# Experts' scales on GpSimd with a power, ahead of placing; totals between the halves of the Gram products

## The chip, the cores and the metric

The kernel runs on one core of a Trainium2 chip. A core has TensorE (PE in the profile, its weight loads PEld), VectorE (DVE), ScalarE (ACT), GpSimd (POOL) and SyncE (SP), each with a queue of its own, and 16 DMA engines. The engines wait for each other by semaphores. The metric is the device time of one execution in microseconds (us), and the median of the runs is compared.

## The reference

Eight batches of 512 tokens, 256 wide, go through a layer norm and an attention whose queries and keys are normed over tokens, so that it can be computed by products of 256x256; then through a layer norm and a mixture of eight experts (two chosen for each token, hidden width 1024) beside a shared layer.

```python
# attention, per batch: x is 512 x 256
Q = x @ Wq.T + bq; K = x @ Wk.T + bk; V = x @ Wv.T + bv
Q = transpose(_l2_norm(Q)); K = _l2_norm(K)
tailor_sum = 1.0 / (L + einsum('bnc,bc->bn', Q, sum(K, axis=-1) + EPS))
matrix = einsum('bmn,bcn->bmc', K, V)
matrix_sum = value_sum + einsum('bnm,bmc->bcn', Q, matrix)
x + gamma * matrix_sum * tailor_sum[:, None, :]
# experts
topk_w, topk_idx = top_k(softmax(flat @ gate_W), 2)
out = 0.5 * gelu(flat @ shared_W + shared_b)
for e in range(8):
    h = gelu(flat @ W1[e] + b1[e])
    out = out + combine[:, e:e + 1] * (h @ W2[e] + b2[e])
```

Each half is followed by a layer norm and added to its input.

## The kernel before

The front part, up to about 230 us, is a software pipeline of steps -1 to 7. In step s batch s+1 enters (layer norm, Gram matrix of its normed tokens), batch s is mixed (256x256 products from the Gram matrix, key and query norms, the mixing matrix), batch s-1 leaves (the attention's result is normed and added, split in a high and a low half of 16 bits, turned, and sent through the shared layer and the gate), batch s-2 is placed (its tokens are counted by expert and get slots in a table), and expert s is prepared. Each engine runs its part of a step in a written order: `step(s)` in the block of that engine, and `last_step()` for step 7.

An expert is prepared so. ScalarE squares W2 (`w2_square`, L1368) and W1 (`w1_square`, L1375) with sums per partition. TensorE adds these over the partitions with one small product of ones (`totals`, L1065, in the bank of the key norms). ScalarE copies the three totals out (`totals_out`, L1352). VectorE makes bounds of them (`expert_bounds`, L1729 to L1732, the last a reciprocal), ScalarE takes the root (`expert_scales`, L1383), and VectorE masks it to a power of two (L1739) and writes the expert's entries of the table `tab` (`expert_tables`, L1740 to L1743). With the scales ScalarE writes the high halves of W2 (`w2_highs`, L1395) and W1 (`w1_highs`, L1389), and VectorE the low halves (`w2_lows`, L1752, and `w1_lows`, L1748). These four each run over 128x2048 elements.

Around them stand, on TensorE: `weigh` (L977, L981), `count` (L1077, L1079), `key_norms` (L990), `cosines` (L998), `totals`, `grams` (L958, 16 matmuls into two halves of a bank), `mix` (L1006), the turning of the leaving tokens (L1043), the shared layer (L534 to L536, L1058), `turn_mix` (L1014), `turn_x` (L967) and `attend` (L1023). `attend` waits for `mixT_out` (L1664) on VectorE, which comes after `w1_lows`. On ScalarE, `spread` (L1272) takes the root for a layer norm, `xf_high` (L1332) writes the high half of the leaving tokens, `xfT_out` (L1338) copies half of the turned ones. On VectorE, `leave` (L1686, L1691) norms the leaving tokens, `xf_low` (L1696) writes their low half, and at the end of step 6 `first_chosen` (L1762 on) reads the places after five batches; it waits for `first_placed`, which GpSimd raises in `keep_places` (L793).

GpSimd places: `place` (L779 to L788) is a chain of 14 small operations, each waiting for the one before; `keep_places` copies the result from batch 4 on; `write_slots` issues indirect DMAs (L797, eight for a batch) into the table. In its queue the batches 0 to 5 follow one another, with the gathers (L811) of blocks 0 and 1 ahead of batch 5 and of blocks 2 and 3 behind it. The blocks' tokens are later turned (L1091) and sent through the experts (L534 to L536 with gelu L1515).

## Time and profile before

| | |
|---|---|
| median of 3 runs | 725.46 us |
| lowest and highest run | 725.3 and 730.57 us |
| the profiled execution's own time | 731.88 us |
| its span, first to last instruction | 730.1 us |
| busy: TensorE, its weight loads | 606.3, 513.5 us |
| busy: VectorE, ScalarE, GpSimd | 465.1, 445.9, 321.3 us |
| mean granted clock of TensorE, as a share of full speed | 0.942 |

A row of a timeline gives the start and the duration of an instruction (or of a few alike, "xN") in us from the start of the span, then engine, source line, operation, output and inputs by name, and shapes. In square brackets stands how long the engine had been idle before it, and what ended that.

### The profile page before, as it was taken

The page shows a single profiled execution, that of the slowest core. Times are in us where ns is not written, and L with a number is a line of the kernel's source. Part 1 is how long each engine was busy: PE and PEld are TensorE (multiplying, and loading weights), DVE is VectorE, ACT ScalarE, POOL GpSimd, SP SyncE. Part 2 cuts the span into 40 slices and gives each one's busy share as a digit, 9 for nine tenths or more (in the row PEclk, how much of TensorE's full clock was granted, in tenths as well). Part 3 has the DMA queues.
Part 4 walks back from the last instruction along what each step waited for, and adds up shares of the span by engine and source line. Part 5 has one row for each costly group of instructions (what it writes and reads, how often), then busy time and mean ns, then how long its engine had stood idle before and what let it go on. Part 6 is the DMA issues. An engine that isn't in the chain of part 4 may idle for free.

```text
span 730.1 us, 16808 instructions
## 1 busy us (share of the span) xinstructions
PE 606.3 (83%) x4903; PEld 513.5 (70%) x4903; DVE 465.1 (64%) x1242; ACT 445.9 (61%) x875; POOL 321.3 (44%) x435
## 2 busy tenths in 40 slices
PE   4778888788867898977969989999999999999400
PEld 3656677677656787855848777889888988888300
DVE  5479899989886545422438766644444445678884
ACT  2657767766745765533635676857656656578743
POOL 4000435645347232644752422334334447674676
PEclk9989999999988999988989999999999999999855
DMA  7553664451453321112112311122212139743438
GB/s 255 181 208 124 192 200 131 160 174 60 123 209 134 99 98 40 48 34 60 53 30 72 94 43 59 46 74 88 75 45 61 44 82 193 155 81 74 98 125 166
DMA packets 45272, 78.25 MB, mean 107 GB/s; under 512 B 16962, under 2 KB 30596, under 8 KB 44804
## 3 DMA queue, kind: packets, MB, share of 16 engines
q1 hardware_dynamic: 33492, 48.19, 20.6%
q0 software_dynamic: 11696, 28.98, 16.5%
q8 instruction: 47, 0.77, 0.5%
q14 instruction: 37, 0.30, 0.2%
HBM read 48.17 MB, written 28.98 MB: 106 GB/s over the span
## 4 chain that ended last, share of the span: by engine, by line
PE 54%; DVE 20%; issue 11%; ACT 6%; another core or an unknown queue 3%; POOL 2%; DMA 2%; DVEq 1%; ACTq 0%; POOLq 0%; SPq 0%
PE banks L534 13%; PE banks L536 12%; PE banks L535 12%; PE banks L1023 3%; PE banks L1193 2%; ACT X L1515 2%; PE banks L958 2%; DVE W L1748 2%; PE banks L1091 2%; DVE W L1752 2%; DVE stage L1981 1%; PE banks L1006 1%; PE banks L981 1%; PE banks L977 1%
## 5 line engine op out<-in xcount | busy, mean ns | idle before, releaser
L1515 ACT ACTIVATE X<-banks,b1T,tab 128x256 f32<-128x256 f32 x256 | 129.2, 554 | 126.7 <-PE banks L536 91.1
L822 POOL DMA_INDIRECT y_rows<-X,tb x72 | 80.6, 1119 | 208.6 <-DVE X L2012 193.5
L1981 DVE SCALAR_TENSOR_TENSOR stage<-X,tab,stage 128x512 f16<-128x512 f32 (+1 forms) x160 | 108.4, 696 | 99.3 <-ACT stage L1521 80.0
L534 PE MATMUL banks<-W,stage 128*128 x576 | 159.7, 277 | 12.0 <-issue 8.6
L536 PE MATMUL banks<-W,stage 128*128 x576 | 159.9, 278 | 5.6 <-issue 5.3
L535 PE MATMUL banks<-W,stage 128*128 x576 | 159.6, 277 | 2.1 <-issue 1.8
L534 PE MATMUL banks<-X,W 128*128 128x256 f16 x512 | 141.5, 276 | 8.8 <-DVE X L1995 7.6
L536 PE MATMUL banks<-X,W 128*128 128x256 f16 x512 | 141.2, 276 | 1.4 <-issue 1.4
L535 PE MATMUL banks<-X,W 128*128 128x256 f16 x512 | 141.3, 276 | 0.3 <-issue 0.3
L1521 ACT ACTIVATE stage<-X,tab 128x512 f16<-128x512 f32 (+1 forms) x160 | 107.1, 679 | 10.7 <-ACT X L1515 6.7
L797 POOL DMA_INDIRECT table<-pay,slot_i x64 | 73.1, 1142 | 58.6 <-PE banks L1023 37.3
L811 POOL DMA_INDIRECT X<-xf_rows,tb x72 | 76.2, 1058 | 32.8 <-issue 21.3
L534 PEld LDWEIGHTS banks<-W,stage 128*128 128x128 f16 x576 | 57.1, 99 | 24.3 <-issue 17.6
L535 PEld LDWEIGHTS banks<-W,stage 128*128 128x128 f16 x576 | 57.2, 99 | 14.3 <-issue 7.0
L536 PEld LDWEIGHTS banks<-W,stage 128*128 128x128 f16 x576 | 57.2, 99 | 12.1 <-issue 5.1
L534 PEld LDWEIGHTS banks<-X,W 128*128 x512 | 50.7, 99 | 17.0 <-issue 10.5
L1995 DVE COPY X<-banks 128x1024 f16<-128x1024 f16 x36 | 24.8, 689 | 57.7 <-remote 50.9
L536 PEld LDWEIGHTS banks<-X,W 128*128 x512 | 50.8, 99 | 9.0 <-issue 2.5
L535 PEld LDWEIGHTS banks<-X,W 128*128 x512 | 50.7, 99 | 6.3
L2005 DVE SCALAR_TENSOR_TENSOR X<-banks,tab,zone 128x512 f32<-128x512 f32 (+1 forms) x39 | 26.7, 694 | 31.0 <-PE banks L536 27.6
L779 POOL TENSOR_TENSOR rank<-counts,zone 128x32 f32<-128x32 f32 x8 | 2.7, 338 | 75.5 <-ACT counts L1358 74.7
L1515 ACT ACTIVATE X<-X,b1T,tab 128x128 f32<-128x128 f32 x64 | 26.4, 483 | 15.6 <-DVE X L1987 15.5
(300 smaller groups left out, 1149.7 us busy)
## 6 DMA issues: line engine op xcount, KB each, us to landing
stage<-in_L_ffn_W SPq DMA_DIRECT2D x10, 1024.0 KB
W<-in_L_ffn_W SPq DMA_DIRECT2D x6, 1024.0 KB, 8.7
X<-in_L_attn_x SPq DMA_DIRECT2D x8, 512.0 KB, 5.5
out<-X SPq DMA_DIRECT2D x8, 512.0 KB
...
```

Of the source, the lines that this page charges most:

```text
L534: pe.matmul(o, lh, rh, start=first, stop=False)
L535: pe.matmul(o, lh, rl, start=False, stop=False)
L536: return pe.matmul(o, ll, rh, start=False, stop=last)
L797: g.indirect_dma_start(out=table, out_offset=bass.IndirectOffsetOnAxis(ap=slot_i[:, b, k, t:t + 1], axis=0), in_=pay[:, b, t, k, :], in_of ...
L811: g.indirect_dma_start(out=xg[:, j % 2 * HALVES + h, :], out_offset=None, in_=xf_rows[0:FIRST * C, :] if j < EARLY else xf_rows, in_offset ...
L822: g.indirect_dma_start(out=y_rows, out_offset=bass.IndirectOffsetOnAxis(ap=tb[:, j % ROWS, h, 1:2], axis=0), in_=y32[:, j % 2 * HALVES + h ...
L1023: mm = pe.matmul(Z_PS[:, t, :], xT[b % 2][:, f, t * P:(t + 1) * P], mixT[:, f, :], start=(f == 0), stop=(f == NF - 1))
L1515: a.activation(tile, tile if joint(j) else PS[m][:, r * BT:(r + 1) * BT], ACT.Gelu, bias=b1T[:, bass.ds(e * NH + 2 * m + r, 1)], scale=tab ...
L1521: a.activation(hhl[:, j % 2, 2 * m:2 * m + 2, 0, span(j, p)], h32[:, m % 2, :].rearrange("p (r n) -> p r n", r=2)[:, :, span(j, p)], ACT.C ...
L1981: v.scalar_tensor_tensor(o[1], src, tab[:, 1, bass.ds(e, 1)], o[0], ALU.mult, ALU.subtract).then_inc(h_low, 1)
L1995: v.tensor_copy(xbT[:, q * NF * 2:(q + 1) * NF * 2, :].rearrange("p a n -> p (a n)"), PS[4][:, :].bitcast(F16)).then_inc(xb_ready, 1)
L2005: v.scalar_tensor_tensor(yq, PS[5 + j % 2][:, :].rearrange("p (h d) -> p h d", h=HALVES)[:, p:p + n, :], tab[:, 2, bass.ds(e, 1)], b2e[:, ...
```

## The change

The scales of expert i move from VectorE and ScalarE to GpSimd. `expert_tables(i)` there is a chain of eleven small operations: the totals are scaled, one `pow` with exponent -0.5 takes the place of reciprocal and root, and a conversion to an integer and back takes the place of the mask. Experts 0 and 1 come ahead of all placing, expert b+2 ahead of `place(b)` for b = 0 to 4, and expert 7 ahead of the first two gathers. ScalarE's splits wait for the seventh operation of the chain. On TensorE the totals' product moves from ahead of the Gram products to between their two halves, in steps 0 to 6. On ScalarE the root `spread(2, ...)` goes ahead of the totals' copy.

```diff
--- before.py
+++ after.py
@@ -22,8 +22,9 @@
 NORMS, TAILOR = 3, 3
 SETUP_V = 14
 LOW_ROW = 32
-EV_BOUNDS, EV = 4, 9
+EV_MASKED, EV = 7, 11
 EXP_MASK = 0x7F800000
+EXP_ONE = float(0x00800000)
 EXP_FLIP = float(0x7F000000)
 BT = 256
 HALVES = BT // P
@@ -124,6 +125,7 @@
         ebnd = sb("ebnd", [P, 4], F32)
         escl = sb("escl", [P, 4], F32)
         einv = sb("einv", [P, 4], F32)
+        eexp = sb("eexp", [P, 4], I32)
         tab = sb("tab", [P, 3, E], F32)
         slot_i = sb("slot_i", [P, B, 2, T], I32)[:, :, :, :]
         pay = sb("pay", [P, B, T, 2, 4], I32)[:, :, :, :, :]
@@ -792,6 +793,28 @@
                 g.wait_ge(placed, PLACES * (b + 1))
                 g.tensor_copy(place_then[:, b - FIRST + 1, :], place_of).then_inc(first_placed, 1)
 
+            def expert_tables(i):
+                e = TURN[i]
+                g.wait_ge(totals_ready, i + 1)
+                g.wait_ge(w1_low, i)
+                g.wait_ge(w2_low, i)
+                settle(g)
+                link = chain(g, expert_steps, EV * i)
+                g.tensor_scalar(ebnd[:, 0:2], etot[:, 0:2], 1e-24, 1.0 / TOP / TOP, ALU.max, ALU.mult).then_inc(expert_steps, 1)
+                link.count[0] += 1
+                link(g.tensor_scalar(ebnd[:, 2:3], etot[:, 0:1], float(D), None, ALU.mult))
+                link(g.tensor_tensor(ebnd[:, 2:3], ebnd[:, 2:3], etot[:, 2:3], ALU.add))
+                link(g.tensor_scalar(ebnd[:, 2:3], ebnd[:, 2:3], 2.0 / TOP / TOP, 1e-24 / TOP / TOP, ALU.mult, ALU.max))
+                link(g.tensor_tensor(escl[:, 0:3], ebnd[:, 0:3], eps[:, 3:4].broadcast_to([P, 3]), ALU.pow))
+                link(g.tensor_scalar(eexp[:, 0:3], escl[:, 0:3].bitcast(I32), 1.0 / EXP_ONE, -0.5, ALU.mult, ALU.add))
+                link(g.tensor_scalar(escl[:, 0:3].bitcast(I32), eexp[:, 0:3], EXP_ONE, None, ALU.mult))
+                assert link.count[0] == EV_MASKED
+                link(g.tensor_scalar(einv[:, 0:3].bitcast(I32), escl[:, 0:3].bitcast(I32), -1.0, EXP_FLIP, ALU.mult, ALU.add))
+                link(g.tensor_scalar(tab[:, 0, e:e + 1], einv[:, 0:1], 1.0 / SX, None, ALU.mult))
+                link(g.tensor_copy(tab[:, 1, e:e + 1], escl[:, 2:3]))
+                link(g.tensor_tensor(tab[:, 2, e:e + 1], einv[:, 1:2], einv[:, 2:3], ALU.mult))
+                assert link.count[0] == EV
+
             def write_slots(b, t):
                 for k in range(2):
                     g.indirect_dma_start(out=table, out_offset=bass.IndirectOffsetOnAxis(ap=slot_i[:, b, k, t:t + 1], axis=0),
@@ -822,12 +845,17 @@
                     g.indirect_dma_start(out=y_rows, out_offset=bass.IndirectOffsetOnAxis(ap=tb[:, j % ROWS, h, 1:2], axis=0),
                                          in_=y32[:, j % 2 * HALVES + h, :], in_offset=None).then_inc(y_stored[j % 2], 16)
 
+            expert_tables(0)
+            expert_tables(1)
             g.wait_ge(table_init, 16)
             for b in range(B - 2):
                 if b + 3 == B:
                     g.wait_ge(cosines_ps, B)
+                    expert_tables(E - 1)
                     gather(0)
                     gather(1)
+                if b + 3 < B:
+                    expert_tables(b + 2)
                 place(b)
                 if b >= FIRST - 1:
                     keep_places(b)
@@ -948,15 +976,16 @@
             mm.then_inc(wqk_turned, 1)
             pe.wait_ge(consts_set, 6)
 
-            def grams(b):
+            def grams(b, lo=0, hi=NF):
                 pe.wait_ge(xs_ready, T * (b + 1))
                 pe.wait_ge(gram_ready, b)
                 pe.wait_ge(u_ready, past(T * (b - 2)))
                 pe.wait_ge(counts_ready, past(b - 2))
-                for i in range(NF):
+                for i in range(lo, hi):
                     for t in range(T):
                         mm = pe.matmul(GRAM_PS[:, i * D:(i + 1) * D], xs[:, t, i * P:(i + 1) * P], xs[:, t, :], start=(t == 0), stop=(t == T - 1))
-                mm.then_inc(gram_ps, 1)
+                if hi == NF:
+                    mm.then_inc(gram_ps, 1)
 
             def turn_x(b, f):
                 pe.wait_ge(xs_ready, T * (b + 1))
@@ -1101,10 +1130,12 @@
                 if mixing is not None:
                     key_norms(mixing)
                     cosines(mixing)
+                if entering is not None:
+                    grams(entering, 0, 1)
                 if i is not None:
                     totals(i)
                 if entering is not None:
-                    grams(entering)
+                    grams(entering, 1, NF)
                 if mixing is not None:
                     mix(mixing)
                 if leaving is not None:
@@ -1375,21 +1406,14 @@
                 a.activation(w1_part(slot(i), 0), staged(i, 0), ACT.Square, accum_out=essq[:, 0:1]).then_inc(w1_squares, 1)
                 a.activation(bsq[:, :], b1T[:, TURN[i] * NH:(TURN[i] + 1) * NH], ACT.Square, accum_out=essq[:, 2:3]).then_inc(w1_squares, 1)
 
-            def expert_scales(i):
-                a.wait_ge(expert_steps, EV * i + EV_BOUNDS)
-                a.wait_ge(w1_low, i)
-                a.wait_ge(w2_low, i)
-                settle(a)
-                a.activation(escl[:, 0:3], ebnd[:, 0:3], ACT.Sqrt, scale=TOP * TOP).then_inc(expert_roots, 1)
-
             def w1_highs(i):
-                a.wait_ge(expert_steps, EV * i + EV_BOUNDS + 1)
+                a.wait_ge(expert_steps, EV * i + EV_MASKED)
                 a.wait_ge(w1_squares, 2 * (i + 1))
                 settle(a)
                 a.activation(w1_part(slot(i), 0), staged(i, 0), ACT.Copy, scale=escl[:, 0:1]).then_inc(w1_high, 1)
 
             def w2_highs(i):
-                a.wait_ge(expert_steps, EV * i + EV_BOUNDS + 1)
+                a.wait_ge(expert_steps, EV * i + EV_MASKED)
                 a.wait_ge(w2_squares, i + 1)
                 settle(a)
                 a.activation(w2_part(slot(i), 0), staged(i, 1), ACT.Copy, scale=escl[:, 1:2]).then_inc(w2_high, 1)
@@ -1414,14 +1438,12 @@
                     w1_square(i)
                 if mixing is not None:
                     q_roots(mixing)
+                if leaving is not None:
+                    spread(2, x1_dev, (x1_mean, T * (leaving + 1)), 0, 1.0 / SX / SX)
                 if i is not None:
                     totals_out(i)
-                if leaving is not None:
-                    spread(2, x1_dev, (x1_mean, T * (leaving + 1)), 0, 1.0 / SX / SX)
                 if mixing is not None:
                     cosines_out(mixing)
-                if i is not None:
-                    expert_scales(i)
                 if leaving is not None:
                     xf_high(leaving)
                 if entering is not None:
@@ -1486,7 +1508,6 @@
                 spread(2, x1_dev, (x1_mean, T * b), 0, 1.0 / SX / SX)
                 cosines_out(b)
                 totals_out(E - 1)
-                expert_scales(E - 1)
                 xf_high(b - 1)
                 mix_scale(b)
                 w1_highs(E - 1)
@@ -1551,6 +1572,7 @@
             spread(2, x1_dev, (x1_mean, T * B), 0, 1.0 / SX / SX)
             a.preload_act_table(ACT.Gelu)
             a.wait_ge(blocks_ready, 1)
+            a.wait_ge(expert_steps, EV * E)
             gelu(0, 0, 2)
             xf_high(B - 1)
             gelu(0, 2, 4)
@@ -1722,27 +1744,6 @@
                 v.tensor_tensor(both, pick[b % 2][0], pick[b % 2][1], ALU.add).then_inc(both_ready, 1)
                 v.tensor_tensor(gap[b % 2], best[1], best[0], ALU.subtract).then_inc(gap_ready, 1)
 
-            def expert_bounds(i):
-                link = chain(v, expert_steps, EV * i)
-                v.wait_ge(totals_ready, i + 1)
-                v.wait_ge(expert_roots, i)
-                link(v.scalar_tensor_tensor(ebnd[:, 2:3], etot[:, 0:1], float(D), etot[:, 2:3], ALU.mult, ALU.add))
-                link(v.tensor_scalar(ebnd[:, 0:2], etot[:, 0:2], 1e-24, None, ALU.max))
-                link(v.tensor_scalar(ebnd[:, 2:3], ebnd[:, 2:3], 2.0, 1e-24, ALU.mult, ALU.max))
-                link(v.reciprocal(ebnd[:, 0:3], ebnd[:, 0:3]))
-                assert link.count[0] == EV_BOUNDS
-
-            def expert_tables(i):
-                e = TURN[i]
-                link = chain(v, expert_steps, EV * i + EV_BOUNDS)
-                v.wait_ge(expert_roots, i + 1)
-                link(v.tensor_scalar(escl[:, 0:3].bitcast(I32), escl[:, 0:3].bitcast(I32), EXP_MASK, None, ALU.bitwise_and))
-                link(v.tensor_scalar(einv[:, 0:3].bitcast(I32), escl[:, 0:3].bitcast(I32), -1.0, EXP_FLIP, ALU.mult, ALU.add))
-                link(v.tensor_scalar(tab[:, 0, e:e + 1], einv[:, 0:1], 1.0 / SX, None, ALU.mult))
-                link(v.tensor_copy(tab[:, 1, e:e + 1], escl[:, 2:3]))
-                link(v.tensor_tensor(tab[:, 2, e:e + 1], einv[:, 1:2], einv[:, 2:3], ALU.mult))
-                assert link.count[0] == EV - EV_BOUNDS
-
             def w1_lows(i):
                 v.wait_ge(w1_high, i + 1)
                 v.scalar_tensor_tensor(w1_part(slot(i), 1), staged(i, 0), escl[:, 0:1], w1_part(slot(i), 0), ALU.mult, ALU.subtract).then_inc(w1_low, 1)
@@ -1882,12 +1883,8 @@
                     x1_stats(leaving)
                 if mixing is not None:
                     inverses(mixing)
-                if i is not None:
-                    expert_bounds(i)
                 if leaving is not None:
                     leave(leaving)
-                if i is not None:
-                    expert_tables(i)
                 if mixing is not None:
                     tailor_factors(mixing)
                 if leaving is not None:
@@ -1920,8 +1917,6 @@
                 inverses(b)
                 tailor_factors(b)
                 leave(b - 1)
-                expert_bounds(E - 1)
-                expert_tables(E - 1)
                 tailor(b)
                 mix_out(b)
                 xf_low(b - 1)
@@ -2071,6 +2066,7 @@
 
             attended(B - 1)
             residual(B - 1)
+            v.wait_ge(expert_steps, EV * E)
             turned_block(0)
             x1_stats(B - 1)
             w2_lows(E - 1)
```

The order of the instructions on GpSimd, where the first batch is placed: before, the program has placing alone there (L779 to L788) and the eight table writes.

```order
L763 IOTA pay 128x64
L779 TENSOR_TENSOR rank<-counts,zone 128x32
L780 TENSOR_TENSOR zone<-zone,counts 128x8
L782 TENSOR_TENSOR zone<-pick,rank 128x32
L767 TENSOR_TENSOR zone<-zone 128x16
```

After the change the table of expert 2 stands there, behind those of experts 0 and 1 (`ebnd`, `escl`, `eexp`, `einv` are its steps, 3 numbers for each partition; the power is L808).

```order
L803 TENSOR_SCALAR ebnd<-counts 128x2
L805 TENSOR_SCALAR ebnd<-counts 128x1
L806 TENSOR_TENSOR ebnd<-ebnd,counts 128x1
L807 TENSOR_SCALAR ebnd<-ebnd 128x1
L808 TENSOR_TENSOR escl<-ebnd,eps 128x3
L809 TENSOR_SCALAR eexp<-escl 128x3
L810 TENSOR_SCALAR escl<-eexp 128x3
L812 TENSOR_SCALAR einv<-escl 128x3
L813 TENSOR_SCALAR tab<-einv 128x1
L814 COPY tab<-escl 128x1
L815 TENSOR_TENSOR tab<-einv 128x1
L780 TENSOR_TENSOR rank<-counts,zone 128x32
```

All of placing, and the table writes behind it, have moved behind these eleven. On VectorE, from the reciprocal of the norms to the low half of the leaving tokens, before:

```order
L1638 RECIPROCAL rk<-kn 128x4
L1729 SCALAR_TENSOR_TENSOR ebnd<-counts 128x1
L1730 TENSOR_SCALAR ebnd<-counts 128x2
L1731 TENSOR_SCALAR ebnd<-ebnd 128x1
L1732 RECIPROCAL ebnd<-ebnd 128x3
L1686 RECIPROCAL cf<-sd 128x4
L1691 TENSOR_SCALAR zone<-X,mv,cf 128x256 x4
L1739 TENSOR_SCALAR escl<-escl 128x3
L1740 TENSOR_SCALAR einv<-escl 128x3
L1741 TENSOR_SCALAR tab<-einv 128x1
L1742 COPY tab<-escl 128x1
L1743 TENSOR_TENSOR tab<-einv 128x1
```

and after, where lines have moved by 17 to 22:

```order
L1660 RECIPROCAL rk<-kn 128x4
L1708 RECIPROCAL cf<-sd 128x4
L1713 TENSOR_SCALAR zone<-X,mv,cf 128x256 x4
L1664 TENSOR_SCALAR gq<-rk,gam_b 128x2
L1665 SCALAR_TENSOR_TENSOR pre<-qsum,rk 128x2
L1666 TENSOR_SCALAR pre<-pre 128x2
L1718 TENSOR_TENSOR zone<-zone 128x4x256
```

Nine operations are gone and nothing has come in their place. On TensorE in step 2, after the change (L1094 is the totals' product, L986 the Gram products, L1027 the cosines, L1035 the mixing):

```order
L1019 MATMUL banks<-ones,W 128x1 x4
L1027 MATMUL banks<-X,W 128x256 x4
L986 MATMUL banks<-W 128x256 x4
L1094 MATMUL banks<-essq,ones 128x3
L986 MATMUL banks<-W 128x256 x4
L1035 MATMUL banks<-b2b,X 128x257 x4
```

Before, the totals' product stood ahead of all eight (one such instruction runs as two passes on the engine, so the trace counts 16).

## Rows read from the trace of the kernel before

**Rows 1.** TensorE's waits, 43 to 233 us: us in total, times, longest.
```profile
PE banks L1023 <- DVE X L1664: 3.8, 6, 1.6
```
**Rows 2.** Timeline of TensorE in step 4.
```profile
121.27 3.72 PE L1023 MATMUL banks<-X 128*128 128x256 f32 x16 [0.26 <-DVE X L1664]
...
130.12 1.97 PE L998 MATMUL banks<-X,W 128*128 128x256 f32 x8
133.69 0.35 PE L1065 MATMUL banks<-essq,ones 128*128 128x3 f32 x2 [1.59 <-ACT kn L1310]
134.08 3.69 PE L958 MATMUL banks<-W 128*128 128x256 f32 x16
137.60 1.90 PE L1006 MATMUL banks<-b2b,X 128*128 128x257 f32 x8
...
146.85 1.35 PE L1023 MATMUL banks<-X,W 128*128 128x256 f32 x5
```
**Rows 3.** Timeline of ScalarE in step 4.
```profile
134.19 0.17 ACT L1352 ACTIVATE counts<-banks 128x3 f32<-128x3 f32 x1 [0.50 <-PE banks L1065]
134.30 0.30 ACT L1272 ACTIVATE sd<-mv,eps 128x4 f32<-128x4 f32 x1
...
136.98 1.06 ACT L1332 ACTIVATE zone<-zone 128x1024 f16<-128x1024 f32 x1 [1.43 <-DVE zone L1691]
...
138.43 1.99 ACT L1395 ACTIVATE W<-stage,escl 128x2048 f16<-128x2048 f32 x1
140.76 1.02 ACT L1338 ACTIVATE zone<-banks 128x1024 f16<-128x1024 f16 x1 [0.34 <-PE banks L1043]
141.68 1.99 ACT L1389 ACTIVATE W<-stage,escl 128x2048 f16<-128x2048 f32 x1
```
**Rows 4.** Timeline of VectorE in step 4.
```profile
135.46 1.38 DVE L1691 TENSOR_SCALAR zone<-X,mv,cf 128x256 f32<-128x256 f32 x4
...
138.39 1.22 DVE L1696 TENSOR_TENSOR zone<-zone 128x1024 f16<-128x1024 f32 x1
...
141.58 2.34 DVE L1752 SCALAR_TENSOR_TENSOR W<-stage,escl,W 128x2048 f16<-128x2048 f32 x1
143.84 2.35 DVE L1748 SCALAR_TENSOR_TENSOR W<-stage,escl,W 128x2048 f16<-128x2048 f32 x1
146.10 0.69 DVE L1664 TENSOR_TENSOR X<-banks,lngb 128x512 f32<-128x512 f32 x1
```
**Rows 5.** Timeline of GpSimd at the end: powers on 4 and 2 elements.
```profile
677.06 1.04 POOL L870 TENSOR_TENSOR pay<-pay,eps 128x4 f32<-128x4 f32 x1
...
720.50 0.72 POOL L882 TENSOR_TENSOR pay<-pay,eps 128x2 f32<-128x2 f32 x1
```
**Rows 6.** Timeline of GpSimd in step 4: first and last of placing.
```profile
131.56 0.25 POOL L779 TENSOR_TENSOR rank<-counts,zone 128x32 f32<-128x32 f32 x1 [1.53 <-ACT counts L1358]
...
135.43 0.82 POOL L788 TENSOR_SCALAR pay<-zone,der 128x4 f32<-128x4 f32 x2 [0.21 <-POOL slot_i L785]
```
**Rows 7.** Timeline of all engines, 221.3 to 224.2 us: VectorE and GpSimd.
```profile
221.43 2.35 DVE L1748 SCALAR_TENSOR_TENSOR W<-stage,escl,W 128x2048 f16<-128x2048 f32 x1
221.60 2.29 POOL L782 TENSOR_TENSOR zone<-pick,rank 128x32 f32<-128x32 f32 x1
```
**Rows 8.** Timelines of GpSimd in step 6 and of VectorE behind it.
```profile
186.76 0.25 POOL L793 COPY zone<-zone 128x8 f32<-128x8 f32 x1 [0.16 <-POOL pay L788]
...
197.86 0.15 DVE L1762 TENSOR_TENSOR zone<-zone 128x8 f32<-128x8 f32 x1
...
202.12 1.42 DVE L1602 BATCH_NORM_STATS2 st<-banks 128x6 f32<-128x256 f32 x4
```
**Rows 9.** Timeline of TensorE in step 2.
```profile
78.97 1.97 PE L998 MATMUL banks<-X,W 128*128 128x256 f32 x8
81.67 0.35 PE L1065 MATMUL banks<-essq,ones 128*128 128x3 f32 x2 [0.72 <-ACT kn L1310]
```
**Rows 10.** The page's costliest groups: GpSimd's table writes, busy us and mean ns.
```profile
L797 POOL DMA_INDIRECT table<-pay,slot_i x64 | 73.1, 1142 | 58.6 <-PE banks L1023 37.3
```

1 line of the change is left out of this document (removed).

## The prediction

> **What bounds the kernel now.** The waits of TensorE over the front part of the kernel (43 to 233 us) come first. They show that in six steps TensorE stands before the attention product L1023 until VectorE has written the mixing matrix with L1664, 3.8 us in all [rows 1]. So the end of each of VectorE's steps sets the pace there. The timeline of TensorE gives the length of a step: L1023 of one step starts at 121.27, of the next at 146.85, so 25.58 us [rows 2]. The timelines of ScalarE and VectorE in the same step show what leads up to that end [rows 3, 4]. ScalarE copies the totals out (L1352, 134.19), splits W2 (L1395, 138.43), copies the turned tokens (L1338, 140.76), and splits W1 (L1389, 141.68). VectorE subtracts the high parts (L1752 at 141.58, L1748 at 143.84), writes L1664 at 146.10, and L1023 starts at 146.85. L1748 needs L1389, whose end is 143.67. Both engines are thus on one path, and the quantity to follow is the start of L1395. It lies 4.24 us after L1352.
>
> The rest of the kernel (tokens through their experts) is not touched, and I take it to shift as a whole with the end of step 7. The profiled execution has a span of 730.1 us and a time of 731.88 us; the median of the runs is 725.46. I add the sum of changes, made in the profiled execution, to the median.
>
> **1. Gram products around the totals.** In steps 3 to 6 TensorE idles 1.59 us before the totals L1065 [rows 2]. Half of the Gram products is half of the way from 134.08 (L958) to 137.60 (L1006): 1.76 us. It fits almost exactly into the hole: L1065 stays where it is, and L1006 starts 1.7 us earlier. In step 2 the totals start at 81.67, 2.70 us after L998 started at 78.97 [rows 9]. L998 occupies 1.75 us (in step 4, 130.12 plus its 1.97 is 132.09, the start of the 1.59 us of idle time, and the last product overlaps by 0.2), so only 0.95 us is free there, and the totals come 0.8 us later. Steps 0 and 1 look like step 2. What gains is L1006, and behind it the turning of the tokens.
>
> **2. VectorE loses nine small operations.** Between the reciprocal of the key norms and L1691 it loses a wait and four operations, and between L1691 and L1696 five. The root that L1691 needs no longer stands behind the totals' copy: it was at 134.30 and can go at 133.6, right after the root before it [rows 3]. L1691 then starts at about 134.15 instead of 135.46 [rows 4], its last tile is done 1.38 later, ScalarE's L1332 (1.52 after L1691's start, and 1.06 long) ends at 136.7, and L1696 starts at 136.8 instead of 138.39: 1.6 us earlier. This is worth nothing by itself, because L1752 and L1748 wait for ScalarE's splits.
>
> **3. GpSimd makes the scales.** Seven operations stand ahead of L1395, one of them the power. GpSimd's linked small operations follow each other at 0.32 us (L779 at 131.56, L788, twelve operations on, at 135.43 [rows 6]); I take 0.33, so six of them take 1.98. The trace has no power on 3 elements: on 2 it takes 0.72 and on 4 it takes 1.04 [rows 5]; I take 0.88 and 0.08 for the link. With 0.4 us from the start of L1352 to GpSimd's first operation and 0.1 to ScalarE, L1395 would start 3.45 after L1352 instead of 4.24. But GpSimd is held where VectorE works with two operands from SBUF: L782 started 0.17 us into L1748 and took 2.29 us instead of 0.25, ending when L1748 did [rows 7]. The power ends at 134.19 + 0.4 + 1.3 + 0.96, about 136.8, just where L1696 (two SBUF operands, 1.22 long) now starts. The two last operations ahead of L1395 then fall behind it: 137.95 + 0.66 + 0.1 = 138.7, or 138.3 if the first of the two slips in ahead. I take 4.25 after L1352, that is no gain; the bounds are 3.45 (no hold: 0.8 gained in each of steps 3 to 6) and 4.75 (0.5 lost). The Trainium skill, page "SBUF — State Buffer", section "Who interferes with whom", says that a VectorE instruction with two SBUF inputs contends with a GpSimd instruction that reads SBUF, and that whoever issues first keeps the port. By that, the power could also hold L1696 back, by up to its own 0.9 us; the two operations behind it would come just as late, L1752 waits for ScalarE and not for L1696, and the sum would stay the same. The rows here agree with GpSimd being held; no row read here shows VectorE held.
>
> **Sum over the steps.** Step 0 has no leaving batch and so no L1696: the split comes when it did, VectorE is through with the mixing earlier: -0.6. Step 1: totals and split 0.8 later, of which VectorE's cover before L1748 takes 0.3: +0.5. Step 2 has the same lateness, but TensorE's turning is a whole us earlier: -0.5. In steps 3 to 6 L1338 no longer waits for TensorE (0.34 in step 4, nothing in 3 and 5, [rows 3]), and L1752 starts earlier: -0.2, -0.25, -0.2, -0.5. Together -1.75; with the bounds of point 3 from -4.5 to +1.5.
>
> **4. Placing is moved behind the scales, and VectorE waits for it.** Every instruction of placing (14 operations) and of its eight table writes now stands behind eleven operations that wait for the totals. In step 6 placing ended with L793 at 186.76+0.25 = 187.0, and VectorE asked for it (first_chosen, L1762) at 197.86: 10.9 us of slack [rows 8]. Now: in step 4 L1352 lies 12.6 us ahead of the end of L1664, so in step 6 it lies at 185.3, less the gains so far 184.1; scales start 184.5, the seven end at 188.4, four more (1.3) at 189.7; placing needs 4.7 (131.56 to 136.25 [rows 6]) and 0.3 for keeping its places. L1752 starts at about 190.5, when three operations are done, and by rows 7 each later one is held: one or two get through between L1752 and L1748, and nine (2.8 us) follow after L1748 ends at about 195.4. Placing ends at 198.5, where VectorE would now come to it at 196.1. This is a stall of 2.4 us. Behind it stand picking, then L1602 at 202.12 without a gap [rows 8], and from its statistics ScalarE's root, its copies and L1626: nothing there absorbs it. The bounds are 0 (small operations not held) and 3.5.
>
> **5. Edits at nothing.** Step 7: its nine operations on VectorE go, but it has to wait for TensorE's mixing there anyway, and the scales' user, the last split, comes after the mixing's scaling. The gathers of blocks 0 to 3 start 4 to 5 us later behind the scales and behind placing; TensorE turns these blocks only behind step 7's shared products and the experts' work after them, which I take as cover enough. If that cover went, it would cost what is over. GpSimd's loop: scales 5.1, placing through L1748 9, first write 0.8 later, eight writes at 0.96 + 0.30: 25.0 of 25.6 us. I add 0.3 for steps in which it falls short.
>
> -1.75 + 2.4 + 0.3 = about +1: 726.5 us.
>
> **The rivals.** (a) No hold, or none that matters: the scales are ready 3.45 after L1352, placing ends in time, steps gain 0.5 to 1.0 each: -2 to -4.5, 721 to 723.5. For it: the collision in point 3 is a matter of 0.1 us. Against: L782's 2.29 us. Chance 0.33. (b) GpSimd becomes the bound of the loop. Its table writes take 1.142 us in the mean over all 64 [rows 10], not 0.96; eight of them with 0.30 between are 11.5 us, and the loop 26.3, which is 0.7 over the step. Then the scales come 0.7 later in each of steps 3 to 6, on top of the stall: +3 to +6, 729 to 731.5, and over 1% where each step's place slides further into the held stretches. It decides from a mean write of 1.05 us on. Chance 0.17. (c) The stall and the steps cancel (placing ends at VectorE's call): within 1 us of before. This is a part of my forecast's range, not a case apart. (d) The power's first use, or a conversion to integers on GpSimd, costs microseconds: eight times 1 to 2 us, 733 to 741. Against it: the powers at the tail take 0.72 and 1.04 us and no more [rows 5]. Chance 0.05. (e) A stretch of lower granted clock or a moved transfer that outweighs all of this: 0.03 either way. GpSimd for small elementwise work is what the Trainium skill advises against ("GPSIMD Engine Reference", section "Engine selection": about twice as slow with two inputs); the rows put the small operations at 0.33 a link, and what matters here is whose queue they stand in.
>
> **How the numbers follow.** My forecast (0.42) gives 724.5 to 728.5, likeliest 726.5. Adding (a) whole down to 721 and (b) up to 731 leaves out less than 2 in 10. A measurement of this kernel tells about 1%, 7.3 us, from no change: 718.2 to 732.7. Nearly all the cases lie within it: same 0.91. Slower by over 1% is (d) and the far end of (b): 0.06; faster only (e): 0.03.
>
> **What would show it.** L1065's wait in steps 3 to 6 gone and L1006 1.7 us earlier after L1023. L1395's distance from the totals' copy: near 4.25 if I am right, 3.45 if (a). Small GpSimd operations of 1 to 2.3 us that end with L1752 or L1748. VectorE idle before the first operation of first_chosen for about 2.4 us, released by GpSimd. If (b): GpSimd's first operation of the scales starts with no idle time before it. I am wrong if the steps between L1023 and L1023 change by over 1 us, or the time after 233 us does.

## The result and the profile after

The changed kernel is slower: 740.95 us in the median of four runs (737.18 to 745.81), against 725.38 us of the kernel before in the same comparison (724.88 to 730.57). The ratio is 1.0168, with an interval of 1.0125 to 1.021. The profiled execution took 741.69 us with a span of 739.3 us; that of the kernel before had 730.1. The trace of the kernel before is of an execution 6.5 us over its median, so the two traces differ by less than the medians do.

I lay the two traces side by side by the starts of the attention product (L1023 before, L1052 after). Steps 3 to 6 took 25.49, 25.58, 25.52 and 25.63 us before; after they take 25.65, 29.61, 30.46 and 28.34. At the end of step 7 the changed kernel is 13.9 us late (236.0 against 222.1), at the end of the span 9.2. So the loss is in the steps. A signal is here the semaphore update that an engine gives with the end of an instruction, and for which others wait. First TensorE's timeline of step 4 in the changed kernel, the counterpart of [rows 2]:

```profile
121.92 3.72 PE L1052 MATMUL banks<-X 128*128 128x256 f32 x16
...
129.40 0.26 PE L1108 MATMUL banks<-zone,ones 128*128 128x40 f16 x4
129.95 1.05 PE L1019 MATMUL banks<-ones,W 128*128 128x1 f32 x8 [0.30 <-issue]
130.87 1.97 PE L1027 MATMUL banks<-X,W 128*128 128x256 f32 x8
133.60 1.97 PE L986 MATMUL banks<-W 128*128 128x256 f32 x8 [0.76 <-issue]
138.58 0.36 PE L1094 MATMUL banks<-essq,ones 128*128 128x3 f32 x2 [3.01 <-ACT kn L1341]
138.81 3.09 PE L986 MATMUL banks<-W 128*128 128x256 f32 x8
```

The totals (L1094) wait 3.01 us although half a Gram product stands ahead of them. ScalarE's timeline of the same stretch says what is late:

```profile
130.32 0.20 ACT L1330 ACTIVATION_READ_ACCUMULATOR W<-banks 128x1 f32 x1
133.25 0.20 ACT L1389 ACTIVATE counts<-banks 128x40 f32<-128x40 f32 x1 [2.73 <-remote]
136.17 0.17 ACT L1336 ACTIVATE kn<-banks 128x2 f32<-128x2 f32 x1 [2.72 <-remote]
136.29 1.91 ACT L1406 ACTIVATE W<-stage 128x2048 f16<-128x2048 f32 x1
...
139.08 0.17 ACT L1383 ACTIVATE counts<-banks 128x3 f32<-128x3 f32 x1 [0.32 <-PE banks L1094]
```

The copy of the counts (L1389) starts 3.6 us after TensorE's counts (L1108) ended, the key norms' (L1336) 5.2 us after L1019 ended. "remote" is the view's word for a release that it can pin to no instruction's end. The trace's semaphore records say more: the signal belongs to L1019's last product, ended at 131.01, and is raised at 136.04. What lies over this stretch is GpSimd's row of eight table writes; its first, second and last from the timeline:

```profile
124.58 1.12 POOL L820 DMA_INDIRECT table<-pay,slot_i  x1 [0.85 <-POOL pay L789]
126.00 0.98 POOL L820 DMA_INDIRECT table<-pay,slot_i  x1 [0.30 <-issue]
...
133.61 0.96 POOL L820 DMA_INDIRECT table<-pay,slot_i  x1 [0.30 <-issue]
```

The same view of ScalarE in the kernel before shows the same thing small. There only four writes lay over the counts (in step 4 from 125.27 to 130.03), and three of the steps 3 to 6 have one such wait. First its timeline in step 3:

```profile
105.65 0.20 ACT L1358 ACTIVATE counts<-banks 128x40 f32<-128x40 f32 x1 [1.28 <-remote]
105.79 0.17 ACT L1305 ACTIVATE kn<-banks 128x2 f32<-128x2 f32 x1
```

then its waits from 90 to 240 us (us in total, times, longest):

```profile
ACT counts L1358 <- remote: 3.9, 3, 1.3
```

and these are the waits of the changed kernel:

```profile
ACT kn L1336 <- remote: 8.7, 3, 4.1
ACT W L1330 <- remote: 4.7, 1, 4.7
ACT counts L1389 <- remote: 4.4, 3, 2.7
```

By the semaphore records, TensorE gave 100 signals between 95 and 262 us of the changed kernel. Of the 44 given while GpSimd issued a DMA, 20 were raised over 0.3 us late, by up to 5.6; of the other 56, none. Before: 18 of 59, and 1 of 51. These counts are good to a few: for 9 of the 44 and 11 of the 59 the trace holds no update of their own.

The rest of the change did what the prediction said. The timeline of step 3 has the power (L808) and the conversion behind it (L809), held under L1718:

```profile
111.49 0.90 POOL L808 TENSOR_TENSOR escl<-ebnd,eps 128x3 f32<-128x3 f32 x1
...
112.33 1.22 DVE L1718 TENSOR_TENSOR zone<-zone 128x1024 f16<-128x1024 f32 x1 [0.89 <-ACT zone L1363]
...
112.48 1.13 POOL L809 TENSOR_SCALAR eexp<-escl 128x3 int32<-128x3 int32 x1
...
114.08 2.00 ACT L1419 ACTIVATE W<-W,escl 128x2048 f16<-128x2048 f32 x1 [1.35 <-POOL escl L810]
```

and VectorE's waits have the stall of step 6:

```profile
DVE zone L1763 <- POOL zone L794: 2.2, 1, 2.2
```

The clock also differs. Stretches of the changed kernel, about a step each (busy us of PE, PEld, DVE, ACT, POOL; granted clock; DMA share; GB/s):

```profile
122.00:152.00 30.00, 23.83 (x138) 19.60 (x138) 22.56 (x75) 18.10 (x34) 19.47 (x35) 0.94 0.49 141
152.00:182.00 30.00, 23.88 (x136) 19.76 (x134) 21.71 (x73) 17.90 (x35) 19.53 (x35) 0.89 0.42 124
```

and step 4 of the kernel before:

```profile
121.00:147.00 26.00, 21.95 (x137) 18.32 (x137) 24.07 (x84) 17.70 (x35) 13.95 (x22) 1.00 0.51 163
```

Before, the clock was 1.00 (2.4 GHz) from step 2 to step 6; after, parts of steps 2, 4 and 5 ran at half of it (1.2 GHz).

### The profile page after: what moved, and what is told of

It reads as the page before. It is cut to its first block, busy times and chain, and to the rows that moved or that the text cites. A ratio compares the mean times of both kernels' runs of the same rounds, so it can differ in the third digit from the quotient of the medians.

```text
span 739.3 us, 16829 instructions
## 1 busy us (share of the span) xinstructions
PE 610.3 (83%) x4903; PEld 519.4 (70%) x4903; DVE 455.3 (62%) x1170; ACT 444.6 (60%) x867; POOL 371.2 (50%) x523
## 4 chain that ended last, share of the span: by engine, by line
PE 55%; DVE 14%; issue 10%; POOL 7%; ACT 6%; DMA 4%; another core or an unknown queue 3%; DVEq 1%; ACTq 0%; POOLq 0%; SPq 0%
PE banks L535 12%; PE banks L537 12%; PE banks L536 12%; PE banks L1052 3%; PE banks L986 2%; PE banks L1224 2%; PE banks L1120 2%; DMA X<-y_rows 2%; ACT X L1536 2%; PE banks L1006 2%; PE banks L1035 1%; PE banks L1225 1%; PE banks L1010 1%; DVE X L2000 1%
## 5 line engine op out<-in xcount | busy, mean ns | idle before, releaser
L834 POOL DMA_INDIRECT X<-xf_rows,tb x72 | 85.5, 1187 | 26.9 <-issue 21.3
L820 POOL DMA_INDIRECT table<-pay,slot_i x64 | 66.3, 1036 | 22.5 <-issue 19.9
L803 POOL TENSOR_SCALAR ebnd<-counts 128x2 f32<-128x2 f32 x8 | 2.7, 335 | 86.9 <-ACT counts L1383 86.9
L1990 DVE COPY X<-banks 128x1024 f16<-128x1024 f16 x36 | 24.7, 685 | 29.4 <-remote 24.3
L986 PE MATMUL banks<-W 128*128 128x256 f32 x128 | 34.8, 422 | 3.2 <-ACT counts L1389 2.4
```

The costliest lines, as they stand in the source:

```text
L820: g.indirect_dma_start(out=table, out_offset=bass.IndirectOffsetOnAxis(ap=slot_i[:, b, k, t:t + 1], axis=0), in_=pay[:, b, t, k, :], in_of ...
L834: g.indirect_dma_start(out=xg[:, j % 2 * HALVES + h, :], out_offset=None, in_=xf_rows[0:FIRST * C, :] if j < EARLY else xf_rows, in_offset ...
L986: mm = pe.matmul(GRAM_PS[:, i * D:(i + 1) * D], xs[:, t, i * P:(i + 1) * P], xs[:, t, :], start=(t == 0), stop=(t == T - 1))
L1990: v.tensor_copy(xbT[:, q * NF * 2:(q + 1) * NF * 2, :].rearrange("p a n -> p (a n)"), PS[4][:, :].bitcast(F16)).then_inc(xb_ready, 1)
```

## The experiments

Theory 1: a GpSimd table write in flight holds TensorE's signals back. Theory 2: TensorE's and ScalarE's new order around the Gram halves makes the loss. Theory 3: GpSimd's longer chain bounds the loop. Three more came up on the way: theory 1b, that moved writes only delay other signals instead; theory C, that the halves cost what they do because a longer hole in TensorE's work lowers its clock; theory S, that a late signal is the halves' cost and the clock only follows. The lateness below is by the semaphore records, the largest in steps 3 to 6 of counts / norms / cosines (where an update is missing, the largest of the rest); "loop" is the length of steps 3 to 6, the clock is that of each of these steps. Ratios are to the kernel before on the same chip. Behind the two rows of the first chip, the rows down to a_whole_gram ran on one chip, those to a_defer, to a_wg_pf_free, to b_gap and to the end on one each; the kernel before took 735, 739, 728, 694 and 729 us on them. Its only trace is that of the first chip. Times are compared only within a chip; lateness, clock and length of steps are read from one trace each, often of different chips. a_late_writes and b_dummy have one run each, with 40 writes in a row in step 7, so only their steps 3 to 6 are read.

| kernel | loop, us | late, us | clock | ratio (interval) |
|---|---|---|---|---|
| before (first chip) | 25.5 25.6 25.5 25.6 | 2.0 / 0.9 / 0 | 1.00 | |
| after (first chip) | 25.7 29.6 30.5 28.3 | 5.2 / 5.0 / 3.3 | 0.89 to 1.00 | 1.0168 (1.0125, 1.021) |
| a_late_writes | 25.3 25.9 25.3 25.9 | 0 / 0 / 0 | 0.93 | not comparable |
| a_place_first | 27.5 27.5 27.4 27.2 | 2.0 / 0.8 / 0 | 0.94 | 1.0124 (1.0059, 1.0189) |
| b_row8 | 30.0 30.0 32.8 31.8 | 0 (two of four missing) / 5.0 / 4.8 | 0.84 to 0.94 | 1.0262 (1.0184, 1.034) |
| a_whole_gram | 32.2 28.6 32.0 25.5 | 4.9 / 5.1 / 3.3 | 0.88 to 1.00 | 1.0181 (1.0123, 1.0239) |
| b_free | 26.0 27.3 27.0 26.8 | 0 / 0 / 0 | 0.93 to 0.94 | 0.9988 (0.9967, 1.001) |
| b_dummy | 24.5 24.6 24.5 24.7 | 0 / 0 / 0 | 1.00 | not comparable |
| a_pf_free | 26.8 27.0 25.3 27.4 | 0.1 / 0 / 0 | 0.94 to 1.00 | 1.001 (0.9985, 1.0035) |
| a_defer | 25.3 27.6 27.5 30.1 | 0.1 / 0 / 0 | 0.89 to 0.94 | 1.0135 (1.0087, 1.0183) |
| after_again | 30.1 27.4 30.4 28.3 | 5.1 / 5.0 / 3.4 | 0.89 to 1.00 | 1.016 (1.0112, 1.0208) |
| b_halves | 28.3 27.0 27.9 27.3 | 1.9 / 0.8 / 0 | 0.87 to 0.88 | 1.0096 (1.0062, 1.013) |
| a_gap | 28.1 27.8 29.2 28.3 | 0.2 / 0 / 0 | 0.88 to 0.94 | 1.0175 (1.0127, 1.0222) |
| a_wg_pf_free | 26.5 27.2 25.4 26.6 | 0.2 / 0 / 0 | 0.94 to 1.00 | 1.0009 (0.9979, 1.0039) |
| b_halves_fill | 25.3 25.3 25.3 25.5 | 0 / 0 / 0 | 1.00 | 1.0077 (1.0048, 1.0107) |
| a_wg_pf | 25.9 24.9 26.1 24.9 | 0 / 0 / 0 | 0.93 and 1.00 | 1.0082 (1.0057, 1.0107) |
| b_gap | 24.5 24.6 24.6 25.0 | 0 / 0 / 0 | 1.00 | 1.0082 (1.0056, 1.0109) |
| after_third | 28.6 30.5 28.8 30.0 | 5.3 / 4.7 / 3.4 | 0.89 to 0.94 | 1.0143 (1.0081, 1.0205) |
| b_halves_again | 27.1 26.9 26.9 25.5 | 1.9 / 0.8 / 0 | 0.87 to 0.93 | 1.0065 (1.002, 1.0111) |
| b_fill_again | 25.4 26.8 25.4 26.3 | 1.9 / 0.8 / 0 | 0.94 to 1.00 | 1.0028 (0.9992, 1.0063) |

### Is it the writes?

**a_late_writes**, the changed kernel:

```diff
                     expert_tables(E - 1)
+                    for late in range(FIRST):
+                        for t in range(T):
+                            write_slots(late, t)
                     gather(0)
...
-                write_slots(b, 0)
-                g.wait_ge(mix_ps, b + 3)
-                write_slots(b, 1)
-                g.wait_ge(z_ps, b + 3)
-                write_slots(b, 2)
-                if b + 3 < B:
-                    g.wait_ge(awk_ps, b + 4)
-                write_slots(b, 3)
+                if b >= FIRST:
+                    for t in range(T):
+                        write_slots(b, t)
```

> The changed kernel, with the table writes of blocks 0 to 4 (40 indirect writes) taken out of the loop and issued in one row in step 7, ahead of the first gather; everything else stands as changed. It computes the same. The end is late by about the 40 writes' 1.26 us each, so only steps 3 to 6 are read. Theory 1 (GpSimd's table writes in flight delay TensorE's signals for the counts, the key norms and the cosines): with no write in flight the three signals come within 0.1 us of their matmuls' ends in steps 3 to 6 (changed kernel: up to 5.2, 5.0 and 3.3 us late), and steps 4, 5 and 6 take 24 to 25.5 us from attend to attend instead of 29.6, 30.5 and 28.3. Theory 2 (the Gram product in halves and ScalarE's new order lengthen the step): the signals may come in time, the steps stay at 28 to 30 us. Theory 3 (GpSimd's longer chain is the bound): less of GpSimd's 10 us a step in writes brings some of it, but the signals stay late.

Its ScalarE in step 4, against [2.73 <-remote] and [2.72 <-remote] above:

```profile
129.37 0.21 ACT L1387 ACTIVATE counts<-banks 128x40 f32<-128x40 f32 x1
129.89 0.17 ACT L1334 ACTIVATE kn<-banks 128x2 f32<-128x2 f32 x1 [0.32 <-PE banks L1017]
130.00 1.91 ACT L1404 ACTIVATE W<-stage 128x2048 f16<-128x2048 f32 x1
```

Every late signal is gone with the writes, and the steps are back at 25.6 us in the mean. Theory 2 doesn't explain the 28 to 30 us, since the halves are still in. GpSimd also has less to do here, so theory 3 falls only with the two runs that follow.

**b_row8**, the kernel before:

```diff
+                g.wait_ge(z_ps, b + 3)
                 write_slots(b, 0)
-                g.wait_ge(mix_ps, b + 3)
                 write_slots(b, 1)
-                g.wait_ge(z_ps, b + 3)
                 write_slots(b, 2)
```

> The kernel before, with nothing of the change, but the first four of each block's eight table writes held until attend, so that all eight go out in one row over the start of the next step (10 us, as in the changed kernel). Theory 1 (writes in flight): the norms and cosines become late as in the changed kernel, by 3 to 5 us, the steps 3 to 6 grow by 2 to 5 us each, and the time is 733 to 742. Theory 2 (halves) and theory 3 (GpSimd's chain with the powers): neither is in this kernel, so 725 to 727, since placing behind the writes has some 20 us of slack in most steps.

It is 18.5 us slower than the kernel before, more than the change itself (15.6), from the place of four writes a step and nothing else. Waits of ScalarE, 90 to 240 us:

```profile
ACT kn L1304 <- remote: 15.2, 3, 5.5
ACT counts L1351 <- remote: 3.4, 1, 3.4
```

**b_dummy**, the kernel before with its loop's writes moved as in a_late_writes, and in their place:

```diff
+                    g.wait_ge(z_ps, b + 3)
+                    for n in range(8):
+                        g.tensor_tensor(idle[:, 4 * n:4 * n + 4], eps[:, 2:3].broadcast_to([P, 4]), eps[:, 3:4].broadcast_to([P, 4]), ALU.pow)
```

> The kernel before, with the table writes of blocks 0 to 4 in one row in step 7 (about 50 us at the end, so only steps 3 to 6 are read), and in their place in the loop, behind attend, eight power operations of GpSimd on 4 elements a partition of some 1.04 us each, whose result nobody reads. Theory 1a (it is the DMA of the write): counts, norms and cosines within 0.1 us of their matmuls, steps 3 to 6 of 24.4 to 25.6 us. Theory 1b (any busy GpSimd, or its power operation, holds TensorE's signals): they are late by 2 to 5 us as with eight writes in a row (there cosines 4.7 us, steps of 30 to 33 us).

```profile
121.62 8.03 POOL L846 TENSOR_TENSOR idle<-eps 128x4 f32<-128x4 f32 x8 [12.05 <-PE banks L1026]
```

Eight microseconds of a busy GpSimd in one row delay nothing: it is the DMA that counts. And the kernel before without writes takes 24.6 us a step. So its own writes seem to cost it 1.0 us in each step of 25.6, by traces of two chips.

**a_whole_gram** (the totals ahead of the whole Gram product again, ScalarE's order too) and **a_place_first** (the changed kernel, `place(b)` and `keep_places(b)` ahead of `expert_tables(b + 2)`):

> The changed kernel with only the Gram halves undone: the totals stand ahead of the whole Gram product again, and ScalarE copies them ahead of its spread. Theory 1 (writes in flight): the writes still go out in one row over the next step's start, so the signals stay late and the time is 738 to 742. Theory 2 (halves): the loss goes, 724 to 728. Theory 3 (GpSimd's chain): 737 to 742.

> The changed kernel with one pair of calls exchanged on GpSimd: placing is put back ahead of the experts' scales; scales, powers and Gram halves stand as changed. Theory 1 (writes in flight): four of each block's eight writes go out behind the scales by about 6 us after the totals, the other four where they were before, so the signals are late as in the kernel before (counts 1.3 to 2.0 us, norms 0.9, cosines 0); the scales come up to 1 us later than in the changed kernel; steps of 25.0 to 26.0 us and 723 to 729 us. Theory 2 (halves): 737 to 741, as changed. Theory 3 (GpSimd's chain): the same work on GpSimd in another order, 735 to 741.

Without the halves the loss stays: 1.0181. So what the halves cost alone (below) does not simply add to what the writes cost. With placing first the lateness is back to that of the kernel before, as theory 1 said, but 1.0124 remains where theory 1 had allowed 0.5% at most above the kernel before (729 us was its upper end, on a kernel of 725). w1_square starts 10.0 us behind attend, as before; the scales come 6.0 us behind the totals' copy instead of 4.3, because GpSimd is still placing, and the clock is 0.94. Theory 1 did not give this part.

### Where could the writes stand?

**b_free** and **a_pf_free** (the latter with placing first as well) take out the waits between the writes:

```diff
-                write_slots(b, 0)
-                g.wait_ge(mix_ps, b + 3)
-                write_slots(b, 1)
...
+                for t in range(T):
+                    write_slots(b, t)
```

> The kernel before with the waits between the pairs of table writes taken out: all eight writes of a block go out behind its placing and end by about 125 us in step 4, ahead of the next step's counts, instead of four of them over the counts and norms. Theory 1 (a write in flight delays TensorE's signals): counts and norms come within 0.1 us, the wait of 1.3 us ahead of the counts' copy goes in steps 3 to 6 and w1_square starts about 1.1 us earlier (9.0 instead of 10.1 behind attend), so 3 to 6 us less than the kernel before. Theory 1b (the writes delay whatever stands beside them, so it only moves): the same lateness falls on turned xf and on the mixed block's signals, 0 to 4 us more than before. Theory 2 (TensorE's order makes the signals late): no change of lateness or time.

> The changed kernel with placing ahead of the experts' scales and without the waits between the pairs of writes: eight writes from about 5 us behind the totals, ending about 127 us in step 4, just ahead of the counts. Theory 1 (writes in flight): no late counts, norms or cosines, w1_square 9.0 us behind attend instead of 10.0, steps about 1 us shorter than with placing first alone (26.4 against 27.4), so 4 to 6 us less than that kernel; still 1 to 2 us a step over the kernel before, since the scales wait 1.6 us for placing. Theory 2 (halves) or 3 (GpSimd's chain): as placing first alone, within 1 us.

In b_free the counts and norms are in time and w1_square starts 1.1 us earlier, as expected, yet steps 4 to 6 are 1.1 to 1.7 us longer than in the trace of the kernel before. The lateness moved: the turned xf's signal is up to 2.4 us late under the longer row, and W2's split to the next attention product takes 9.8 to 11.2 us instead of 8.4. That is theory 1b. a_pf_free takes the changed kernel's loss back whole: 1.001. Its halves are still in.

**a_defer** (a block's writes behind the next step's scales, ahead of its placing) and **a_gap**:

> The changed kernel with the writes of a block moved behind the next step's scales and ahead of its placing (block 4 apart: it is placed ahead of the scales, and its last four writes go out behind the last cosines). The scales stay as early as in the changed kernel, and no write of blocks 0 to 3 is in flight over counts, norms or cosines. Theory 1 (writes in flight): signals within 0.1 us in steps 3 to 5 (one or two late in step 7), steps of 25 to 26 us, 4 to 8 us more in step 7 at most; the loop ends about 8 us earlier than in the changed kernel, and the time is within 1% of the kernel before. Theory 3 (GpSimd's chain is the bound): placing is 11 us later than in the changed kernel and the counts' copy waits for it, no gain on the changed kernel.

> The changed kernel with one wait moved: the last four of a block's eight table writes wait for the next step's cosines instead of for attend and the next step's first product. Nothing of the change is undone. Theory 1 (writes in flight): the first four end ahead of the norms, so norms and cosines are in time, counts late by 1 us at most; the last four go beside the totals, which may be late by 1 to 3 us; steps 4 to 6 of 25.5 to 28 us, and 3 to 9 us less than the changed kernel beside it. Theory 3 (GpSimd's chain is the bound): a wait more on GpSimd ahead of the scales can only lengthen it, 0 to 8 us more than the changed kernel.

```diff
                 write_slots(b, 0)
-                g.wait_ge(mix_ps, b + 3)
                 write_slots(b, 1)
-                g.wait_ge(z_ps, b + 3)
+                if b + 3 < B:
+                    g.wait_ge(cosines_ps, b + 4)
                 write_slots(b, 2)
-                if b + 3 < B:
-                    g.wait_ge(awk_ps, b + 4)
                 write_slots(b, 3)
```

Both miss. Counts, norms and cosines are in time in both up to step 6. But in a_defer the row now lies over the first products of a step, whose signals are 1.6 to 3.2 us late (theory 1b again), and the counts' copy starts only when placing is done (134.58 in step 4, behind an end of 134.48): w1_square stands 11.6 us behind attend in step 4 and 12.4 in steps 5 and 6, instead of 9.0. In a_gap the scales wait behind the last four writes (6.6 us behind the totals' copy instead of 4.3). GpSimd is busy for some 19.5 us in a step (the stretches above), and these two runs fit theory 3: once the writes are out of the way of the signals, they stand in the way of its own chain.

**a_wg_pf_free** leaves only the scales on GpSimd (whole Gram, placing first, no waits between writes); **a_wg_pf** keeps the waits. **after_again** and **after_third** are the changed kernel once more, on the chips of the runs beside them.

> Of the change only the scales on GpSimd stay: the whole Gram product behind the totals, placing ahead of the scales, and the table writes in one row right behind the scales, ended ahead of the next counts. Theory 1 (writes in flight), with the halves costing 0.8 us in each step in which the norms are in time: totals copied 2.8 us behind w1_square instead of 3.57, 3 to 6 us less than the same kernel with halves (there 1.001 of the kernel before), so ratio 0.992 to 0.998. Theory 1b (the writes only move their delay to other signals): ratio 1.000 or above.

> Of the change only the scales on GpSimd stay: whole Gram product, placing ahead of the scales, the writes' waits as in the kernel before. From the runs: scales 1.1 to 1.7 us later than before (they wait for placing), the early four writes go out behind the scales, counts and norms late as before (2.0 and 0.85 us). Theory 1 with theory C (writes and clock): steps of 25.5 to 27 us, 0 to 8 us over the kernel before, ratio 1.000 to 1.010, against 1.012 with the halves in it. If the scales on GpSimd were worth what they were put there for: below 0.998.

> The changed kernel once more, as the measure for the runs beside it, since the kernel before took 735 to 739 us on the chips of the other runs and 725 on that of the result. Theory 1 (writes in flight): signals late by 2 to 5 us and steps 4 to 6 of 28 to 30.5 us as in its first trace, ratio to the kernel before 1.012 to 1.021. Theories 2 and 3 expect the same of it.

At 1.0009 and 1.0082 the scales on GpSimd gain nothing. With placing ahead they come 5.1 us behind the totals' copy.

### What do the halves cost?

**b_halves** is the kernel before with the Gram halves and ScalarE's order alone; **b_halves_fill** computes the second half twice from step 2 on, which changes nothing but TensorE's idle time:

```diff
-                for i in range(lo, hi):
+                again = b > 2 and hi == NF
+                for i in list(range(lo, hi)) + [NF - 1] * again:
```

> The kernel before with one part of the change alone: the totals between the halves of the Gram product, ScalarE's spread ahead of its copy of the totals. Theory 1 (writes in flight make the loss): writes stay where they were, counts 2.0 and norms 0.85 us late as before, totals copied 0.8 us later in steps 0 to 2 and at the same time in steps 3 to 6, 0 to +3 us in all (ratio 1.000 to 1.005). Theory 2 (halves make the loss): most of the 1.7% is here, ratio 1.010 or more.

> The kernel before with the Gram halves, and from step 2 on the second half of the Gram product computed twice over (8 more matmuls, about 1.9 us of TensorE, the same result). The extra work falls in the hole of 2 us ahead of the turning of xf, so TensorE stands still 1.9 us less in one place. Theory C (the longer hole makes the chip lower TensorE's granted clock, and that is the halves' cost): the clock stays at 1.00 in steps 3 to 6 or falls for 3.4 us instead of 6.8, the steps take 25.6 to 27 us instead of 27.0 to 28.3, and the kernel with more work is 2 to 6 us faster than with the halves alone (ratio to the kernel before 1.001 to 1.007). Theory S (the signal of the turned xf, 2.3 us late under the writes, is the cost, and the clock only follows): the steps stay at 27 to 28.3 us, ratio 1.009 or more; if the product were on the path that sets the step, 7 us more on top.

The halves alone cost 1.0096, where I had expected 1.000 to 1.005. The run with filler was on a chip on which no signal is late. Both were therefore repeated beside the changed kernel on one chip that has late signals:

> The changed kernel. The lateness tells the kind of chip. With late signals (the kernel before at 725 to 740): ratio 1.012 to 1.021 as before. Without them (the kernel before at some 694): theory 1 with theory C (writes and clock) expects the steps of the run without writes in the loop, 25.3 to 25.9 us, granted clock 0.93 in each step, counts, norms and cosines in time, and the loop to end 1 to 4 us later than before, with first_chosen's stall of 2 us on it: ratio 1.000 to 1.008. Theory 3 (GpSimd's chain is the bound) expects 1.015 or more on this kind too.

> The Gram halves alone in the kernel before. With late signals: 1.006 to 1.013 as in its first run. Without them: the hole ahead of the totals moves behind the mix and joins that of the turned xf. Theory C (clock): granted clock 0.87 to 0.94 in steps 3 to 6 and steps of 25.5 to 26.5 us. Theory S (the signal is the cost): clock 1.00, steps as with the hole filled, 25.3 us.

> The Gram halves with the second half computed twice from step 2 on. On the last chip: clock 1.00 in steps 2 to 6, 25.3 us a step, the same number as the kernel before had with late signals. Theory C: faster than the halves alone by 1 to 5 us on either kind of chip, although it does 11 us more work on TensorE. Theory S: 0 to 3 us slower than the halves alone on the kind without late signals.

TensorE in step 3 of b_halves_again:

```profile
112.45 1.90 PE L1007 MATMUL banks<-b2b,X 128*128 128x257 f32 x8
116.52 1.81 PE L1044 MATMUL banks<-ident,zone 128*128 128x128 f16 x16 [2.17 <-issue]
119.17 0.40 PE L534 MATMUL banks<-zone 128*128 128x264 f16 x1 [0.84 <-DVE zone L1704]
119.36 0.43 PE L535 MATMUL banks<-zone 128*128 128x264 f16 x1
```

and in step 3 of b_fill_again:

```profile
113.48 1.90 PE L1008 MATMUL banks<-b2b,X 128*128 128x257 f32 x8
115.76 1.05 PE L1045 MATMUL banks<-ident,zone 128*128 128x128 f16 x16 [0.38 <-issue]
117.69 0.29 PE L534 MATMUL banks<-zone 128*128 128x264 f16 x1 [0.88 <-DVE zone L1705]
117.81 0.28 PE L535 MATMUL banks<-zone 128*128 128x264 f16 x1
```

In b_halves_again TensorE stood 2.17 us ahead of turning xf and 0.84 behind it, and the shared products after that take 0.43 us instead of 0.28: half clock. With the hole filled they take 0.28. Stretches of the two kernels, granted clock in the third column from the end:

```profile
98.00:125.00 27.00, 23.79 (x137) 19.80 (x136) 23.79 (x83) 17.90 (x34) 12.24 (x22) 0.87 0.54 157
```

```profile
97.00:123.00 26.00, 23.40 (x144) 19.81 (x145) 24.14 (x84) 17.74 (x35) 13.87 (x22) 1.00 0.54 163
```

No xf signal is late in b_halves_again, so no late xf signal stands behind the fall of the clock (theory S): with the hole it fell, with the hole filled it stayed at 1.00 in this step. Over the ten runs of each, the mean granted clock was 0.925 with the halves alone and 0.938 with filler. With 9 us more work (five times eight products, 1.8 us) the loop ended 2.6 us earlier (225.5 against 228.1), and steps 3 to 5 took 77.6 us against 80.9. In the times, 1.0028 and 1.0065, the intervals overlap: traces and clocks speak for theory C, the times alone don't show it. The Trainium skill, "TensorE: Matmul & The Clock Gate", Part 1 ("The HAM clock gate"), has it that TensorE's default is the lower clock and activity releases it; the two stretches agree, with 0.87 where TensorE idled and 1.00 where it worked through.

On the chip without late signals **b_gap** (a_gap's wait in the kernel before) ran:

> The kernel before with one wait moved: the last four of a block's table writes wait for the next step's cosines instead of for attend and the next first product. Theory 1 (writes in flight): counts and norms within 0.1 us, w1_square 9.1 us behind attend instead of 10.1; the last four go beside the totals and the mix, whose signals have more slack, and placing with the early four comes 6 us later, beside the end of the step. If nothing there is hit, steps of 24.5 to 25 us and 3 to 6 us less than the kernel before (ratio 0.992 to 0.996); if the early four now hit the turned xf or the mixed block (theory 1b), 1.000 to 1.010.

Its steps 3 to 5 are at 24.5 to 24.6 us, but on this chip the run says nothing about late signals. It is slower all the same: the last writes and gathers slide (first gather at 218.8 us, 213.9 in the trace of the kernel before), and step 7 takes 25.5 us (24.2 there). No version beat the kernel before.

## Why the prediction was wrong

**Point 1, Gram halves: wrong in the steps that counted.** In steps 0 to 2 the totals' copy came 0.8 us later as said (3.57 behind w1_square instead of 2.79). For steps 3 to 6 I read 1.59 us before L1065 as room [rows 2]. It was not TensorE's own: step 2, in which no write lies over the counts, had 0.72 [rows 9], and b_dummy has 0.72 in each of steps 2 to 5; the rest was the late counts and norms. Filling it did not shorten the path, it joined TensorE's idle time into one hole ahead of the turned xf. With that the clock fell, to 0.87 in b_halves_again. The cost alone was 1.0065 and 1.0096, where I had counted a small gain, within the -1.75 us of all steps.

**Point 2: right.** L1718 starts 2.51 us after the totals' copy (109.82 in step 3), where L1696 stood 4.20 behind it [rows 3, 4].

**Point 3: right.** The power takes 0.90 us for my 0.88, L809 is held to 1.13 us under L1718, and the split stands 4.20 to 4.40 us behind the totals' copy in steps 3 to 6 (forecast 4.25). The port rule of the Trainium skill, "SBUF — State Buffer", "Who interferes with whom", fits L809's row.

**Point 4: right as far as it went.** VectorE waits 2.2 us for the kept places (forecast 2.4).

**Point 5 is the step that failed.** "Edits at nothing" counted the eight writes for GpSimd's own time: "eight writes at 0.96 + 0.30", +0.3. They do take that and less than before (mean 1.036 us; 1.142 in [rows 10]), and GpSimd has 4.91 us to spare in step 4. What I did not price is where they land. Behind the scales and placing all their waits were already met, so eight went out in one row over the next step's counts, norms and cosines. From the traces of four kernels: without writes in the loop a step takes 24.6 us before (b_dummy) and 25.6 after (a_late_writes); with them 25.6 and 28.5 (means of steps 3 to 6). So of 2.96 us a step, 1.0 is the change itself (the totals' 0.8 and the clock fit it) and 2.0 the writes' new place. Four steps of 2.96 are 11.8 of the 13.9 us. The four traces are of three chips, and the changed kernel's mean step was 28.5, 29.0 and 29.4 us in its three traces, so the shares are an estimate, good to about 1 us. The kernel before had shown it: three waits on "remote" ahead of the counts' copy, 3.9 us in all, that I had not followed up.

**The rivals.** (a) and (d) were not met. (b) GpSimd as the bound: no in the changed kernel (4.91 us idle in step 4 and 1.66 in step 3), while a_defer and a_gap fit it. (e), a lower clock, was part of it, and I gave it 0.03; a result slower by over 1%, as this one, had 0.06 in all. That the rest shifts as a whole with the end of step 7 was wrong too: the turning of the experts' blocks (L1091, now L1120) is 16.1 us late at 327 us and 11.4 at 414, and the end 9.2. No run here settles why.
